# Loading and splitting two weight matrices of the feed-forward stage during the last two halves of the attention stage

## The reference, cut to what matters

```python
xn = _layernorm(x, axis=-1)
x = x + _L0_attn_ref(xn, W_q, W_k, W_v, W_o, beta_param) + _L0_ffn_ref(xn, ..., router_w, router_b, wq, wk, wv, wo, w1, w2, ln1, ln2)
```

```python
weights = (x @ router_w)[..., 0] + router_b[0]
topv, topi = jax.lax.top_k(weights, k)          # k = 1024
sel_idx = jnp.sort(topi[:, :kc], axis=1)        # kc = 1023
x_sel = x[bidx, sel_idx]
hn = rmsnorm(x_sel, ln1)
q = rope(heads(hn @ wq), pos_sel)
kk = rope(heads(hn @ wk), pos_sel)
v = heads(hn @ wv)
```

## Time and profile before

| | |
|---|---|
| median of 3 runs | 1976.8 us (1975.86 to 1978.17) |
| the profiled execution | 1976.38 us |
| its span, first to last instruction | 1974.6 us |
| attention stage, opening, rest | up to 1284 us, 1284 to 1423 us, from 1423 us |
| TensorE busy | 1865.2 us (94%) |
| VectorE busy | 1440.8 us (73%) |
| ScalarE busy | 874.0 us (44%) |
| GpSimd busy | 149.3 us (8%) |

### The profile page before, as it was taken

The page is one execution under the profiler, slowest core; times in us unless marked ns, Lnnn a source line. Parts: engine busy times, 40 slices in busy tenths (PEclk is TensorE's granted clock), DMA queues, the critical chain, the costliest instruction groups (busy, mean ns, idle before and its releaser), DMA issues. The chain is left out here.

```text
span 1974.6 us, 72364 instructions
## 1 busy us (share of the span) xinstructions
PE 1865.2 (94%) x32380; PEld 1580.6 (80%) x32380; DVE 1440.8 (73%) x3478; ACT 874.0 (44%) x1494; POOL 149.3 (8%) x179
## 2 busy tenths in 40 slices
PE   6999999999999999999999999759899999988998
PEld 6888888888888888888888888547676766667997
DVE  6888888888888777877777776466587887876222
ACT  4343444434344443434343444135587777764110
POOL 1000000000000000000000000041100000001000
PEclk9999999999999999999999999769999999999999
DMA  4112111211211121111111110146500000015000
GB/s 145 46 46 75 59 46 52 77 51 46 72 62 36 38 60 41 35 57 40 41 35 57 46 36 24 34 160 186 161 13 12 12 13 23 12 41 162 13 12 22
DMA packets 65141, 108.47 MB, mean 55 GB/s; under 512 B 4721, under 2 KB 25217, under 8 KB 64833
## 3 DMA queue, kind: packets, MB, share of 16 engines
q1 hardware_dynamic: 59056, 84.69, 13.7%
q0 software_dynamic: 5776, 19.15, 3.0%
HBM read 59.26 MB, written 27.26 MB: 44 GB/s over the span
## 5 line engine op out<-in xcount | busy, mean ns | idle before, releaser
L409 POOL TENSOR_TENSOR As<-T 128x512 f32<-128x512 f32 x64 | 82.3, 1286 | 1176.6 <-DVE T L817 1176.6
L1997 DVE CUSTOM_DVE_ANT_0 Sm<-Sp,mc 128x1023 f32<-128x1023 f32 x128 | 155.6, 1216 | 10.1 <-DVE r L1249 2.8
L1895 ACT ACTIVATE Sm<-Sm,least 128x1023 f32<-128x1023 f32 x128 | 146.8, 1147 | 14.3 <-DVE least L1997 13.5
L2043 PE MATMUL Sp<-KS,QS 128*128 128x512 f32 x256 | 95.2, 455 | 35.5 <-DVE least L1997 29.5
L464 ACT ACTIVATE Pq<-Pq 128x1024 f32<-128x1024 f32 x64 | 68.0, 1062 | 121.2 <-DVE Pq L786 120.9
L444 ACT ACTIVATE QT<-proj 128x512 f32<-128x512 f32 x64 | 38.1, 595 | 181.8 <-PE proj L992 181.8
L1947 DVE COPY PTs<-Tp 128x512 f32<-128x512 f32 x128 | 88.1, 688 | 40.5 <-PE Tp L2055 40.1
L427 ACT ACTIVATE DV<-proj 128x512 f32<-128x512 f32 x64 | 38.3, 598 | 159.8 <-PE proj L1002 159.8
L2264 PEld LDWEIGHTS Sp<-QS,KS 128*128 128x128 f32 x768 | 97.3, 194 | 8.8 <-issue 3.6
L1868 ACT ACTIVATE PTs<-Tp 128x512 f32<-128x512 f32 x128 | 76.2, 595 | 63.5 <-PE Tp L2051 62.3
L2264 PE MATMUL Sp<-QS,KS 128*128 128x256 f32 x768 | 99.2, 286 | 5.4 <-DVE QS L2249 2.7
(11 more groups left out here) (332 smaller groups left out, 4831.2 us busy)
## 6 DMA issues: line engine op xcount, KB each, us to landing
VS<-DV SPq DMA_DIRECT2D x64, 264.0 KB, 3.9
xin<-in_x SPq DMA_DIRECT2D x32, 512.0 KB, 4.8
out_rows<-xu SPq DMA_DIRECT2D x64, 256.0 KB, 2.0
mask_columns<-x1T SPq DMA_DIRECT2D x16, 512.0 KB
xs<-in_w SPq DMA_DIRECT2D x16, 512.0 KB, 4.0
xe<-in_x SPq DMA_DIRECT2D x15, 512.0 KB, 3.6
QT<-in_wqT SPq DMA_DIRECT2D x1, 1024.0 KB, 6.0
KT<-in_wkT SPq DMA_DIRECT2D x1, 1024.0 KB, 9.0
```

The costliest lines, as they stand in the source:

```text
L409: pool.tensor_tensor(As[:, :], T1[:, :], T2[:, :], ALU.add).then_inc(s_as, 1)
L1895: act.activation(Sm[:, h % 4, 0:KC], Sm[:, h % 4, 0:KC], ACT.Exp, bias=least[:, h % 4:h % 4 + 1], scale=-1.0, accum_out=rsum[:, b, h:h + 1 ...
L1997: dve.tensor_tensor_reduce(Sm[:, h % 4, 0:KC], Sp[h % 2][:, 0:KC], mc[:, b, 0:KC], 1.0, 3.0e38, ALU.add, ALU.min, least[:, h % 4:h % 4 + 1])\
L2043: ins = pe.matmul(Sp[h % 2][:, u * 512:u * 512 + 512], QS[:, h, :], KS[:, h, u * 512:u * 512 + 512], start=True, stop=True)
```

## The change

Three buffers of 1 MB, `held`, are allocated outside both stages. In the attention stage they are the high parts of its `wk` and `wq` and the low part of its `wq`; afterwards they become what `QS`, `qst` and `mc` were, and in the MLP the two tiles `gT`.

In half 30 SyncE loads the next key weights into `xin` and the next query weights into `xn`. In half 31 ScalarE makes both high parts and VectorE the low part of the key weights. The opening then loads only `wq` (for its low part) and `wv`, makes the query weights' low part without waiting for ScalarE, and has the value weights' low part made behind `angles`, ahead of `roots` and `turns`. The number of subtractions and copies stays the same; one load of 1 MB is added (`wq` is read twice).

```diff
+        key_high, query_high, key_low = [weight(held, n, G) for n in (HIGH[KEY], HIGH[QUERY], LOW)]
+        wq = (key_high, key_low)
+        wk = (query_high, sb("wk_low", [P, G, D], F32R)[:, :, :])
+        next_raw = [t[:, :, :, :].rearrange("p a b n -> p (a b) n") for t in (xin, xn)]
...
+            def next_weight(n, d):
+
+                sp.dma_start(next_raw[n], d.rearrange("(c p) n -> p c n", p=P)).then_inc(s_cw[n], 16)
+
...
+                if m == NB - 2:
+                    sp.wait_ge(s_xu, NB)
+                    next_weight(KEY, wk_d)
+                    got(sp, "XT1", NB - 3)
+                    next_weight(QUERY, wq_d)
                 if stage1:
                     shift_v(m, 1 - p)
...
+            def next_high(n):
+                act.wait_ge(s_cw[n], 16)
+                copy((key_high, query_high)[n], next_raw[n]).then_inc(s_ch, 1)
+
...
                 neg_a(m, 0)
                 p_turned(m, 0)
+                if not stage1:
+                    for n in (KEY, QUERY):
+                        next_high(n)
...
+            def next_low():
+                dve.wait_ge(s_ch, 1)
+                dve.tensor_tensor(key_low, next_raw[KEY], key_high.bitcast(F32), ALU.subtract).then_inc(s_cl, 1)
+
...
+                if not stage1:
+                    next_low()
                 row_max(m, 1)
                 less_max(m, 1)
...
-                for n, (dst, _, d) in enumerate(weights):
-                    sp.dma_start(dst, d.rearrange("(c p) n -> p c n", p=P)).then_inc(s_wd[n], 16)
+                for n, d in enumerate((wq_d, wv_d)):
+                    sp.dma_start(raw[n], d.rearrange("(c p) n -> p c n", p=P)).then_inc(s_wd[n], 16)
...
                 act.activation(cos[:, 0, 0:1], ident[:, 0:1], ACT.Sin)
-                high_w(KEY)
                 high_h(0)
-                high_w(QUERY)
-                high_w(VALUE)
+                value_high()
...
+                def query_low():
+                    dve.wait_ge(s_wd[0], 16)
+                    dve.tensor_tensor(qlow[:, :, :], raw[0], high[QUERY].bitcast(F32), ALU.subtract).then_inc(s_low, 1)
+
+                def value_low():
+                    dve.wait_ge(s_high, 1)
+                    dve.tensor_tensor(vlow[:, :, :], raw[1], vhigh[:, :, :].bitcast(F32), ALU.subtract).then_inc(s_low, 1)
...
                 moments(0, 1)
                 scaled(0)
-                low_w(KEY)
                 moments(1, 2)
                 low_h(0)
-                low_w(QUERY)
+                query_low()
                 angles(0)
+                value_low()
                 roots(0)
                 turns(0)
-                low_w(VALUE)
```

78 lines of the change are left out of this document (39 added, 39 removed).

## The result

| | before | changed |
|---|---|---|
| median | 1975.95 us (1975.29 to 1978.17, 6 runs) | 1966.68 us (1964.26 to 1969.86, 6 runs) |
| ratio | | 0.9952 (95%: 0.9941 to 0.9962) |
| span of the profiled execution | 1974.6 us | 1962.4 us |
| TensorE busy | 1865.2 us (94%) | 1860.4 us (95%) |
| VectorE busy | 1440.8 us (73%) | 1440.1 us (73%) |

The change makes the kernel 9.3 us faster in this comparison. The forecast was 1971.9 us, the range 1970.2 to 1974.8: the sign was right, the gain was about twice the one predicted, and the time lies 3.5 us under the lower end of the range.

What follows compares the result with a forecast made beforehand. VectorE's queue up to the first key rotation was taken to bound the opening, TensorE what follows; 1976.4 - 4.94 + 0.05 = 1971.5, plus 0.4 for the runs' median, gave 1971.9 us, range 1970.2 to 1974.8.

Steps and rivals of the forecast that it cites:

- the start: Opening, gather of tile 0: rows in use at 1293.61 as before, SyncE's queue still full of weights, so no gain.
- step 4: Opening, value subtraction: weights land at 1301.43 by queue place, VectorE stands 0.66 us, step ends at 1305.59.
- Steps 1 to 3: Opening, VectorE: key subtraction gone, 1.25 us won; query subtraction follows without standing 4.27 us; `angles` ends at 1302.72.
- the value weights come earlier: Opening: value weights land by 1300.8, the 0.66 us of standing go, gain 5.60 us, 1971.2; counted with the forecast.
- The rival that they come late: Opening: value weights land later than by queue place, centre 1974.4 us with gain 2.4 us; chance 0.22.
- Step 5: Opening, VectorE: `roots` and `turns` cost 3.37 us, so the first key rotation starts at 1308.96 instead of 1313.90.
- The last halves: Attention halves 30 and 31: loads and ScalarE's copies cost nothing, VectorE's subtraction before the row maximum is charged 0.05 us.

Runs made afterwards that it cites:

- `wo` or `wv` first: Changed kernel plus an unused 1 MB load of the output or the value weights, first in SyncE's queue in the opening: 0.9983 and 0.9979 of before.
- before again: The kernel before, unaltered, profiled a second time: ratio 1.0000 to before.
- buffers: Kernel before with the change's shared held buffers only, all loads, copies and subtractions in the opening in the old order: 1.0005 of before.
- order: Kernel before with only the value weights' subtraction moved ahead of the roots: 0.9994 of before.
- attention part: Kernel before with shared buffers and the early loads, copies and key subtraction added in the last two attention halves, opening still doing everything: 0.9999 of before.
- changed three times: The changed kernel, unaltered, in three comparisons with the kernel before: 0.9952, 0.9976 and 0.9952.
- old order: Changed kernel with the value weights' subtraction moved back behind the scaled sines: 0.9959 of before.
- `wk` last: Changed kernel plus an unused 1 MB load of the key weights, last in SyncE's queue in the opening, behind the value weights: 0.9967 of before.
- three subtractions: Changed kernel with the key weights' subtraction done three times instead of once in the last attention half: 0.9976 of before.
- second comparison: The changed kernel, unaltered, measured again against the kernel before: 0.9976, 5.4 us under before.

## Why the prediction was right, and where it was wrong

The path was right: the chain through VectorE's queue sets the opening, TensorE is not in the way, the stretch behind the first rotation shifts as a whole (18.43 us in both kernels), and the moved work is hidden. What failed were two terms, the start (put at nothing) and step 4 (mis-sized), both on how loads in one queue land, and the width of the range.

**The start.** "SyncE's queue is still full of weights beside it, so I leave it there": this failed. The first gather took 7.6 to 7.7 us in the changed kernel's three profiles, 7.1 to 7.9 in all that load something else first, and 8.5 to 8.7 in all that load `wk` first. That is 0.91 us more gain. It is not the amount of loads (with a third load last it is 7.80, with `wo` or `wv` first 7.06 and 7.48), but that load.

**Steps 1 to 3** held: 1.25 us predicted for the key subtraction, 1.28 measured by adding one; the angles end 9.14 us behind the first statistics, 9.11 predicted.

**Step 4** was mis-sized: "so by place they come at 1301.43", and from that "0.66 us of standing". No standing was left: the angles ended 0.03 us later than predicted and the subtraction followed at once, so 0.63 us were won. The rows of before showed second place at 16.35 us behind the gather's issue, but that was second place behind `wk`; behind other weights it is 12. I had this case ("the value weights come earlier") at a gain of 5.60 and 1971.2 us. The rival that they come late did not come true.

**Step 5**: roots and turns took 3.12 us, not 3.37. The difference is one instruction, the first `rs` of the roots: 0.43 us in the kernel before (at 1308.59) and 0.17 in the changed one (at 1302.73). Together 0.91 + 0.63 + 0.25 = 1.79 us more than the 4.94 of the sum.

**Where the gain is from.** Five profiles with the old opening (before, before again, buffers, order, attention part) have 28.86 us of gather and chain in the mean, six with the new one (changed three times, old order, `wk` last, three subtractions) 22.22: 6.6 us. The six lie within 22.06 to 22.38, the five from 27.72 to 29.58, so the 6.6 is known to about 1 us only. The subtraction alone is worth 1.3 of them, and nothing when the load is there (28.83 without it): VectorE then stands for the query weights in its place. So the load is what pays: without taking it out of the opening, moving the subtraction gains nothing. A load of other weights in first place costs 3.0 us (25.1 and 25.4, one profile each); the 3.6 beyond that are the key weights' own.

**The last halves.** Two DMAs and two copies at nothing: right. For the subtraction the prediction charged 0.05 us, since 1.19 us of slack cover even a wait for GpSimd. It was GpSimd that waited, and the maximum was 0.03 us late. The rule of the Trainium skill (SBUF — State Buffer, Who interferes with whom) agrees with the trace: 3.39 us for an addition that takes 1.27 alone. With three subtractions both sides are seen: the first shuts GpSimd out (3.40 us), and GpSimd's addition then lengthens the second to 3.25 us where 2.28 are its own.

**The rest of the miss.** The part behind the first rotation is 0.4 us shorter in the changed kernels (656.7 against 657.1 in the mean, where the ScalarE wait is 5.0); I can't say from what. The start is the same in the mean, 1287.0 in the five with the old opening and 1286.8 in the six. So the profiles give 7.0 us, a ratio of 0.9965, and the three comparisons 0.9952, 0.9976 and 0.9952, 0.9960 in the mean. Of the 4.4 us by which the first comparison's gain beat the forecast some 2 are the opening's and the rest's, and 2.3 have no cause in the profiles: scatter between comparisons. The second comparison alone, with 5.4 us, would have looked like a hit; that would have been luck, since the 4.94 us were wrong all the same. The prediction allowed 1 us of scatter for a run; the start alone lies anywhere from 1283.50 to 1291.52 us, for the same code 1285.08 and 1291.25. The right sum, 1969.8, lies 0.4 us under the range; and to reach the measured 1966.68 from there takes the 2.3 us of scatter and 0.85 more, by which the kernel before had itself come down, from 1976.8 us (3 runs) to 1975.95 (6 runs), when the two were compared.

**Open.** Why the load of the key weights, alone of the four (each stood first in some kernel), delays the load behind it and the gather beside it. The runs show that it isn't the number of loads or the buffer that it goes to (`wv` and `wo` went to the same one), nor its place alone (second in the queue it delays too, by less). It isn't the chip: on the one where `wv` stood first, the kernel before, profiled again, has the late load too. Where its data lie in memory was not tried.

The landings in the traces narrow it down. Each load lands in 16 pieces. In the five kernels that load `wk` first and whose 16 landings are all on record, 14 pieces of the second load are in by 13.9 us behind SyncE's first instruction of the stage, and the last comes at 16.0 to 17.9. In the seven with another load first, the last one comes at 12.8 to 13.8. The opening behind `wk` follows that one piece: from its landing to the first rotation it is 12.2 to 12.5 us in all five, with the last piece at 16.0 where gather and chain took 27.72, and at 17.9 where they took 29.58. So it is one or two pieces that are late and not the load, and how late they are also makes the old opening scatter more than the new one. Why one piece lags is not shown.

## What to carry to other kernels

When a load is removed, don't take the remaining loads' landing times from their places in the old queue: put an unused load back, in each place and from another tensor, and see which of them waits. A subtraction that fills a wait for a load is worth nothing until the load goes as well; ask what each is worth without the other. And for effects of a few us in 2000, compare segments between two marks in the timeline, in more than one profile: for the new opening they agreed within 0.3 us (22.06 to 22.38), for the old one within 1.9 (27.72 to 29.58), where the gain by medians came out as 9.3, 5.4 and 8.2 us.

## What the hardware showed unasked

A load of one particular tensor put the next load in the queue in use 4.5 to 4.6 us later than loads of two other tensors of the same size in the same place did (16.57 against 12.08 and 11.97 us), and made the gather beside it 1.1 to 1.6 us longer (8.61 against 7.48 and 7.06). One or two of the next load's 16 pieces were late (the last at 17.3 us, against 12.8), the others not. One wait in the MLP was 8.0 us in all four profiles on one chip and 5.0 in all twelve on two others, for either kernel. The stretch up to the first gather took 1283.5 to 1291.5 us in the 18 profiles, 1285.1 and 1291.3 for the kernel before and 1283.5, 1286.0 and 1287.1 for the changed one.
